# The mixing of a unit stands one step later, next to the scores, in two attention stages

## The chip, the cores and the metric

The kernel runs on one core of one Trainium2 chip. The metric is the device time of one execution in microseconds (us). All tensors are float32; the projections split each operand into a rounded high part and the rest (fp32r) and sum the products.

## The reference

The program is a small vision tower on 64 images of 36 tokens, 192 channels: patch embedding, a causal attention with 12 heads of 64 columns, a block with a norm, an attention with 12 heads of 16 columns and an MLP, a second attention with 12 heads of 16 columns and a distance bias, and a mixture of experts. The change touches the two 16-column attentions only. What one of them computes:

```python
qkv = x @ w_qkv.T + b_qkv                       # x: (64, 36, 192)
q, k, v = qkv.reshape(B, N, 3, 12, 16)...       # 12 heads of 16
scores = einsum('bhnd,bhmd->bhnm', q, k) * 16 ** -0.5 + bias
attn = softmax(scores, axis=-1)
out = einsum('bhnm,bhmd->bhnd', attn, v)        # the mixing
return out.transpose(...).reshape(B, N, 192) @ w_proj.T + b_proj
```

The first of them (named attn2) has no bias in the scores and a layer norm ahead of it; the second (attn3) has the bias.

## The kernel before, in words

Both stages are `narrow_stage` (L563). The 2304 tokens are taken as 32 units of two images (72 tokens), four units to a group, so 8 groups of 288 tokens. Each engine has its program written out by hand, as a loop over 35 steps k; engines meet by semaphores only. Every engine works through its own list in order.

For unit k the work goes through the engines like this:

- TensorE `scores(k)` (L802): 8 matmuls, q against a block-diagonal copy of the keys (tiles keys_a, keys_b; L813). Before the first unit of a group it waits for the 12 transfers that fill these tiles (L806).
- VectorE `take_scores(k)` (L1011): row maximum and, in attn2, the subtraction (L1023, L1025). In attn3 it adds the bias (L1017), takes the maximum (L1021), and GpSimd subtracts (`shift`, L722).
- ScalarE `exponentiate(k)` (L927), VectorE `sum_up(k)` (L1031, L1036), GpSimd `normalise(k)` (L715).
- TensorE `turn(k)` (L817): 4 transposes (L823); ScalarE `copy_turned(k)` (L934) brings them to prob_t.
- TensorE `mix(k)` (L827): 8 matmuls of prob_t with the block-diagonal values (L839, 8 instructions, told as 8 pairs of load and matmul); ScalarE `copy_z(k)` (L944) brings the result to z_t.
- TensorE `project_out(t)` for a token tile t of 128 (L848, L849), VectorE `add_residual(t)` (L1040).

At step k the TensorE issues scores of unit k, the transposes of unit k-2, a share of the next group's input work, the output projection of a finished tile, and last the mixing of unit k-2. The next group's input work is spread over the four steps of a group: transposes of x (L768, L769) at the first, the projections of q and k (L779 to L783, twice) at the second, the third projection and the first values (L795 to L799) at the third, the other values at the fourth.

The key tiles are filled by the SyncE queue (`spread_keys_a`, L646, and `spread_keys_b`, L656). It waits until ScalarE has copied the keys (tile k_a, L911 in attn2 and L913 in attn3, which follows the second of the two projections at a group's second step), issues 8 transfers for keys_a (L653), then 4 for keys_b (L659), then 9 for the values (L673). In attn3 the same queue also loads weights for the last stage (L1800, L1802 each group; ten transfers at L1783 to L1790 once, behind the keys of group 2). Groups are counted from 0 here; "the keys of group 4" are those that unit 16 waits for.

Of the kernel before, what the change touches and what calls it, by code (L numbers as in the profile page):

```python
# [562 lines left out]
def narrow_stage(nc, psum, ident, neg_half, name, h_tok, y_tok, w, out_ws, c2_scale, qk_bias, bias_hk,  # L563
# [4 lines left out]
    groups, units = TOK // WIDE, TOK // UNIT  # L568
# [19 lines left out]
    with Sems(nc, name) as S, ExitStack() as ctx:  # L588
# [29 lines left out]
        def scores_ps(k):  # L618
            return bank(2 + k % 2)[:, 0:HEADS * SEQ].rearrange("p (h n) -> p h n", h=HEADS)
# [139 lines left out]
        def _(pe):  # L759
# [42 lines left out]
            def scores(k):  # L802
                g, u = k // per_group, k % per_group
                if u == 0:
                    pe.wait_ge(S["qk_copied"], 3 * g + 3)
                    pe.wait_ge(S[f"keys_ready{g % 2}"], 16 * 12 * (g // 2 + 1))  # L806
                if k >= 2:
                    pe.wait_ge(S["scores_taken" if bias_hk is not None else "shifted"], k - 1)
                ps = scores_ps(k)
                for q, keys, h0, h1 in ((q_a, keys_a, 0, 8), (qk_b, keys_b, 8, HEADS)):  # L810
                    for a in range(2):
                        at = u * UNIT + a * SEQ
                        last = nc.tensor.matmul(ps[64 * a:64 * a + 64, h0:h1, :], q[g % 2][:, at:at + 64],  # L813
                                                keys[g % 2][:, :, at:at + SEQ], start=True, stop=True)
                last.then_inc(S["scores_done"], 1)

            def turn(k):  # L817
                pe.wait_ge(S["normalised"], k + 1)
                if k >= 2:
                    pe.wait_ge(S["turned_copied"], k - 1)  # L820
                flat = prob[k % 3][:, :, :].rearrange("p h n -> p (h n)")
                for n in range(4):
                    last = nc.tensor.transpose(bank(4 + k % 2)[0:3 * SEQ, n * P:n * P + QP],  # L823
                                               flat[:, n * 3 * SEQ:(n + 1) * 3 * SEQ], ident[0:QP, 0:QP])
                last.then_inc(S["turned"], 1)
# [32 lines left out]
            for k in range(steps):  # L858
                g, j = k // per_group + 1, k % per_group
                if k < units:  # L860
                    scores(k)
                if 2 <= k < units + 2:
                    turn(k - 2)
                if g < groups:
                    if j == 0:
                        transpose_x(g)
                    elif j == 1:
                        project(g, 0)
                        project(g, 1)
                    elif j == 2:  # L870
                        project(g, 2)
                        values(g, 0)
                    else:
                        values(g, 1)
                        values(g, 2)
                for t in ready_tiles(k):
                    project_out(t)
                if 2 <= k < units + 2:
                    mix(k - 2)

        @block.scalar
        def _(act):
            def round_x(g):
                ts = new_tiles(g)
                n, at = len(ts) * P, ring_span(ts)
                act.wait_ge(S["x_transposed"], g + 1)
                if prenorm:
                    ga, gb, ba, bb = norms[g * len(norms) // groups]
                    act.wait_ge(S["x_split"], g)
                    nc.scalar.activation(aff_a[:, 0:n], bank(0)[:, 0:n], ACT.Identity, bias=ba, scale=ga  # L890
                                         ).then_inc(S["x_affine"], 1)
                    nc.scalar.activation(aff_b[:, 0:n], bank(1)[0:DB, 0:n], ACT.Identity, bias=bb, scale=gb
                                         ).then_inc(S["x_affine"], 1)
                    act.wait_ge(S["x_affine"], 2 * g + 2)
                    nc.scalar.activation(a_hi[:, at], aff_a[:, 0:n], ACT.Copy).then_inc(S["x_rounded"], 1)
                    nc.scalar.activation(b_x[0:DB, at], aff_b[:, 0:n], ACT.Copy).then_inc(S["x_rounded"], 1)
                else:
                    nc.scalar.activation(a_hi[:, at], bank(0)[:, 0:n], ACT.Copy).then_inc(S["x_rounded"], 1)
                    nc.scalar.activation(b_x[0:DB, at], bank(1)[0:DB, 0:n], ACT.Copy
                                         ).then_inc(S["x_rounded"], 1)  # L900

            def copy_qk(g, c):
                act.wait_ge(S["qk_done"], 3 * g + c + 1)
                if c == 1 and g >= 1:
                    act.wait_ge(S[f"keys_ready{(g - 1) % 2}"], 16 * 12 * ((g - 1) // 2 + 1))
                if c != 1 and g >= 2:
                    act.wait_ge(S["scores_done"], per_group * (g - 1))
                out = (q_a[g % 2], k_a, qk_b[g % 2])[c][:, 0:WIDE]
                scale = (0.25, 1.0, c2_scale)[c]
                if qk_bias is None:  # L910
                    ins = nc.scalar.activation(out, bank(c % 2)[:, 0:WIDE], ACT.Copy, scale=scale)  # L911
                else:
                    ins = nc.scalar.activation(out, bank(c % 2)[:, 0:WIDE], ACT.Identity,  # L913
                                               bias=qk_bias[:, c:c + 1], scale=scale)
                ins.then_inc(S["qk_copied"], 1)

            def copy_v(g, n):
                act.wait_ge(S["v_done"], 3 * g + n + 1)
                if g >= 1 and n == 0:
                    act.wait_ge(S[f"values_ready{(g - 1) % 2}"], 16 * 9 * ((g - 1) // 2 + 1))  # L920
                m = 3 * SEQ if n < 2 else 2 * SEQ
                nc.scalar.activation(v_tok[0:m, n, :], bank((n + 1) % 2)[0:m, 0:D], ACT.Copy
                                     ).then_inc(S["v_copied"], 1)

            def exponentiate(k):
                act.wait_ge(S["shifted"], k + 1)
                nc.scalar.activation(prob[k % 3][:, :, :], prob[k % 3][:, :, :], ACT.Exp  # L927
                                     ).then_inc(S["exp_done"], 1)

            def copy_turned(k):  # L930
                act.wait_ge(S["turned"], k + 1)
                if k >= 2:
                    act.wait_ge(S["mixed"], k - 1)
                nc.scalar.activation(prob_t[k % 2][:, :, :, :], turned_ps(k)[0:3 * SEQ, :, :, 0:SEQ], ACT.Copy  # L934
                                     ).then_inc(S["turned_copied"], 1)

            def copy_z(k):
                act.wait_ge(S["mixed"], k + 1)
                over = k * UNIT + UNIT - 1 - z_ring
                if over >= 0:  # L940
                    act.wait_ge(S["out_done"], over // P + 1)
                at = (k * UNIT) % z_ring
                n = min(UNIT, z_ring - at)
                ins = nc.scalar.activation(z_t[:, :, at:at + n], z_ps[:, :, 0:n], ACT.Copy)  # L944
                if n < UNIT:
                    ins = nc.scalar.activation(z_t[:, :, 0:UNIT - n], z_ps[:, :, n:UNIT], ACT.Copy)
                ins.then_inc(S["z_copied"], 1)

            round_x(0)
            for c in range(3):  # L950
                copy_qk(0, c)
            for n in range(3):
                copy_v(0, n)
            for k in range(steps):
                g, j = k // per_group + 1, k % per_group
                if 1 <= k <= units:
                    exponentiate(k - 1)
                if 2 <= k < units + 2:
                    copy_turned(k - 2)
                if g < groups:  # L960
                    if j == 0:
                        round_x(g)
                    elif j == 1:
                        copy_qk(g, 0)
                        copy_qk(g, 1)
                    elif j == 2:
                        copy_qk(g, 2)
                        copy_v(g, 0)
                    else:
                        copy_v(g, 1)  # L970
                        copy_v(g, 2)
                if side and j == 1 and g <= groups:
                    side.round_step(act, g - 1)
                if 2 <= k < units + 2:
                    copy_z(k - 2)

        @block.vector
        def _(dve):
# [1109 lines left out]
```

## Time and profile before

| | us |
|---|---|
| Median of 3 runs | 1170.06 |
| Lowest and highest | 1166.44, 1171.95 |
| The profiled execution | 1165.79 |
| Its span in the profile | 1164.0 |
| Mean granted TensorE clock | 0.938 of full speed |
| PE (matmul) busy | 1013.6 (87%) |
| DVE, ACT, POOL busy | 561.9, 395.4, 319.6 |
| attn2: first scores to last projection | about 354 to 496 |
| attn3: the same | about 646 to 803 |

PE is the TensorE with its matmuls, PEld its weight loads (they run beside the matmuls), DVE the VectorE, ACT the ScalarE, POOL the GpSimd, SP the SyncE. A matmul's end is modelled, so successive matmuls overlap in the listing and a busy PE is not a PE at its peak. "Idle before, releaser" is the time in which an engine did nothing ahead of an instruction, and what ended that. The releaser "issue" means that the profile shows nothing that the engine waited for; a wait for a transfer may be put down there.

### The profile page before, as it was taken

How to read it: one execution, taken by the hardware profiler on the slowest of the kernel's cores; microseconds unless marked ns; L12 is line 12 of the kernel's file. 1: busy time of each engine (PE TensorE's matmuls, PEld its weight loads, DVE VectorE, ACT ScalarE, POOL GpSimd, SP SyncE). 2: the span in 40 equal slices, each digit the busy share in tenths (PEclk: the TensorE clock that was granted, in tenths of full speed). 3: DMA queues.
4: the chain of work that ended last, by engine and by line, in shares of the span. 5: the costliest groups of instructions: out<-in, count | busy, mean ns of one | idle time of the engine just before them, and what ended most of it. 6: DMA issues, size and time to landing. Idle time of an engine off the chain costs nothing. (4 is left out here: it accounts for less than half of the span.)

```text
span 1164.0 us, 21593 instructions
## 1 busy us (share of the span) xinstructions
PE 1013.6 (87%) x8306; PEld 925.2 (79%) x8306; DVE 561.9 (48%) x1489; ACT 395.4 (34%) x882; POOL 319.6 (27%) x349
## 2 busy tenths in 40 slices
PE   6879998999847999868998678976999999999997
PEld 6768888888735777758997466865999999999996
DVE  2225454555544666457331355654444454545444
ACT  1245554555413455323442344542212121111110
POOL 4424343443441222224223465663000000000000
PEclk9999999999977899879998898986999999999999
DMA  9711010101001111000000142210000000000000
GB/s 294 219 39 24 24 33 24 33 23 29 29 4 27 26 29 28 16 1 1 1 1 22 48 115 66 65 47 3 1 1 12 1 11 1 11 1 12 1 11 11
DMA packets 40757, 39.08 MB, mean 34 GB/s; under 512 B 21072, under 2 KB 32208, under 8 KB 40656
## 3 DMA queue, kind: packets, MB, share of 16 engines
q1 hardware_dynamic: 38528, 33.38, 10.3%
q10 hardware_dynamic: 2128, 4.34, 1.3%
q8 instruction: 66, 1.08, 0.4%
q14 instruction: 35, 0.29, 0.1%
HBM read 21.76 MB, written 1.77 MB: 20 GB/s over the span
## 5 line engine op out<-in xcount | busy, mean ns | idle before, releaser
L1485 ACT ACTIVATE moe_silu<-psum 128x384 f32<-128x384 f32 x108 | 53.2, 492 | 273.7 <-PE psum L76 266.3
L1389 POOL TENSOR_TENSOR moe_rstd<-moe_var_eps,neg_half 128x3 f32<-128x3 f32 x6 | 5.1, 851 | 349.5 <-DVE moe_var_eps L1584 349.5
L715 POOL TENSOR_TENSOR attn_prob<-attn_prob,attn_recip 100x432 f32<-100x432 f32 x64 | 58.3, 912 | 132.2 <-DVE attn_recip L1036 132.2
L839 PEld LDWEIGHTS psum<-attn_prob_t,attn_values 108*64 108x64 f32 x1024 | 66.6, 214 | 24.5 <-issue 10.5
L839 PE MATMUL psum<-attn_prob_t,attn_values 108*64 108x36 f32 x1024 | 74.1, 293 | 10.5 <-DMA attn_values<-attn_v_tok 6.2
L1555 DVE TENSOR_TENSOR moe_hid_pair<-psum,moe_silu 128x384 f32<-128x384 f32 x72 | 40.1, 557 | 87.3 <-PE psum L76 87.3
L813 PE MATMUL psum<-attn_keys_a,attn_q_a 128*64 128x288 f32 x256 | 51.2, 480 | 35.4 <-issue 23.2
L1571 DVE SCALAR_TENSOR_TENSOR moe_acc<-psum,moe_coef,moe_acc 128x192 f32<-128x192 f32 x144 | 59.7, 418 | 44.9 <-PE psum L1439 44.5
L1439 PE MATMUL psum<-w_dn,moe_hid_pair 128*128 128x192 f32 x288 | 73.4, 337 | 6.3 <-DVE moe_acc L1571 6.3
L72 PE MATMUL psum<-moe_x_a_hi,w_gu_a_hi 128*128 128x384 f32 x216 | 76.2, 353 | 0.0
L235 POOL TENSOR_TENSOR attn_prob_x<-attn_prob,attn_recip 100x864 f32<-100x864 f32 x32 | 52.6, 1643 | 76.4 <-DVE attn_recip L517 76.4
L74 PE MATMUL psum<-moe_x_a_hi,w_gu_a_lo 128*128 128x384 f32 x216 | 72.9, 338 | 0.0
L73 PE MATMUL psum<-moe_x_a_lo,w_gu_a_hi 128*128 128x384 f32 x216 | 72.9, 338 | 0.0
L76 PE MATMUL psum<-moe_x_b,w_gu_b_lo 128*128 128x384 f32 x216 | 72.9, 337 | 0.0
L75 PE MATMUL psum<-moe_x_b,w_gu_b_hi 128*128 128x384 f32 x216 | 72.8, 337 | 0.0
L1031 DVE TENSOR_REDUCE attn_row_sum<-attn_prob 100x12 f32<-100x432 f32 x64 | 38.5, 602 | 63.2 <-ACT attn_prob L927 62.9
L1439 PE MATMUL psum<-w_dn_mid,moe_hid_pair 128*128 128x192 f32 x288 | 69.0, 335 | 0.0
L1236 ACT ACTIVATE mlp_hid<-psum,columns 128x384 f32<-128x384 f32 x72 | 39.9, 581 | 54.2 <-PE psum L76 36.3
L1439 PEld LDWEIGHTS psum<-w_dn,moe_hid_pair 128*128 128x128 f32 x288 | 49.0, 190 | 10.9 <-DVE moe_acc L1571 10.7
L1439 PEld LDWEIGHTS psum<-w_dn_mid,moe_hid_pair 128*128 128x128 f32 x288 | 47.0, 189 | 4.9 <-DVE moe_acc L1571 3.7
L1726 PE MATMUL psum<-embed_w_tok,embed_patches 128*128 128x192 f32 x216 | 39.5, 341 | 10.3 <-DMA embed_w_tok<-in_tok_w 5.8
L1726 PEld LDWEIGHTS psum<-embed_w_tok,embed_patches 128*128 128x128 f32 x216 | 36.4, 197 | 13.1 <-DMA embed_patches<-in_x 7.2
(318 smaller groups left out, 2698.3 us busy)
## 6 DMA issues: line engine op xcount, KB each, us to landing
embed_patches<-in_x SPq DMA_DIRECT2D x18, 384.0 KB, 23.1
attn_v<-attn_v_tok SPq DMA_DIRECT2D x16, 216.0 KB
attn_values<-attn_v_tok SPq DMA_DIRECT2D x96, 27.0 KB
attn_keys_a<-attn_k_a SPq DMA_DIRECT2D x128, 18.0 KB, 1.8
raw_a<-in_w_gu_dram SPq DMA_DIRECT2D x8, 288.0 KB, 3.2
raw_b<-in_w_gu_dram SPq DMA_DIRECT2D x16, 144.0 KB, 3.2
y<-moe_y SPq DMA_DIRECT2D x6, 288.0 KB
attn_keys_b<-attn_qk_b SPq DMA_DIRECT2D x64, 18.0 KB, 1.8
```

What stands on the lines that cost most here:

```text
L72: nc.tensor.matmul(out, w.a_hi[:, cols], x.a_hi[:, toks], start=True, stop=False)
L73: nc.tensor.matmul(out, w.a_hi[:, cols], x.a_lo[:, toks], start=False, stop=False)
L74: nc.tensor.matmul(out, w.a_lo[:, cols], x.a_hi[:, toks], start=False, stop=False)
L75: nc.tensor.matmul(out, w.b_hi[:, cols], x.b[:, toks], start=False, stop=False)
L76: return nc.tensor.matmul(out, w.b_lo[:, cols], x.b[:, toks], start=False, stop=True)
L235: nc.gpsimd.tensor_tensor(prob_x[k % 2][:, :, :, :], prob[k % 3][:, :, :].rearrange("p h (a n) -> p h a n", a=1) .to_broadcast([QP, HEADS, ...
L715: nc.gpsimd.tensor_tensor(pr, pr, recip[k % 2][:, :].rearrange("p (h a) -> p h a", a=1) .to_broadcast([QP, HEADS, SEQ]), ALU.mult).then_in ...
L839: last = nc.tensor.matmul(ps[r:r + 64, n // 2, a * SEQ:(a + 1) * SEQ], v[:, n, :], prob_t[k % 2][:, n, a, :], start=True, stop=True)
L1439: last = nc.tensor.matmul(down_ps(n), hid(gr)[:, c, t * MT:(t + 1) * MT], w, start=(m == 0), stop=(m == len(terms) - 1))
L1485: nc.scalar.activation(silu[c % 2][:, :], bank(2 * (c % 2))[:, 0:MW], ACT.Silu).then_inc(S["silu_done"], 1)
L1571: ins = nc.vector.scalar_tensor_tensor(out=acc[:, t, :], in0=down_ps(n), scalar=scalar, in1=h_tok[:, 3 * i + t, :] if e == 0 else acc[:, t ...
L1726: last = nc.tensor.matmul(out_bank(t), patches[:, t, c, :], w_tok[:, c, :], start=(c == 0), stop=(c == chunks - 1))
```

## The change

In the TensorE's list the mixing moves from the end of step k, where it took unit k-2, to the place right behind the scores of step k, where it takes unit k-3. In the ScalarE's list the copy of its result moves from the end of the step to the place behind the exponential, with the same unit k-3. Nothing else is edited: as many instructions, the same operands, the same semaphores. The lists of DVE, POOL and SP are the same.

```diff
@@ TensorE
                 if k < units:
                     scores(k)
+                if k >= 3:
+                    mix(k - 3)
                 if 2 <= k < units + 2:
                     turn(k - 2)
...
                 for t in ready_tiles(k):
                     project_out(t)
-                if 2 <= k < units + 2:
-                    mix(k - 2)
@@ ScalarE
                 if 1 <= k <= units:
                     exponentiate(k - 1)
+                if k >= 3:
+                    copy_z(k - 3)
                 if 2 <= k < units + 2:
                     copy_turned(k - 2)
...
-                if 2 <= k < units + 2:
-                    copy_z(k - 2)
```

On the TensorE, at the end of a group's last step and the start of the next group in attn2, before and with the change (L799 ends the last values, L813 are scores, L839 is the mixing, L823 the transposes of the probabilities, L768 those of x):

```order
 L799 MATMUL psum<-w_qkv_b_lo,attn_b_x 72x192
-L839 MATMUL psum<-attn_prob_t,attn_values 64x36 x8
-L813 MATMUL psum<-attn_keys_a,attn_q_a 64x288 x2
-L813 MATMUL psum<-attn_keys_b,attn_qk_b 64x144 x2
+L813 MATMUL psum<-attn_keys_a,attn_q_a 64x288 x2
+L813 MATMUL psum<-attn_keys_b,attn_qk_b 64x144 x2
+L839 MATMUL psum<-attn_prob_t,attn_values 64x36 x8
 L823 MATMUL psum<-ident,attn_prob 108x100 x4
 L768 MATMUL psum<-ident,attn_x_hat 128x128
```

The mixing that stood ahead of a group's first scores, and so ahead of their wait for the key tiles, now stands behind them.

On the ScalarE, in the same steps of attn2 (L922 are copies of values, L944 the copy of a mixing, L927 an exponential, L934 the copy of the transposed probabilities, L890 the first work on the next group's x):

```order
-L944 ACTIVATE attn_z_t<-psum 128x2x72
-L927 ACTIVATE attn_prob<-attn_prob 100x432
-L934 ACTIVATE attn_prob_t<-psum 108x288
-L922 ACTIVATE attn_v_tok<-psum 108x192
-L922 ACTIVATE attn_v_tok<-psum 72x192
-L944 ACTIVATE attn_z_t<-psum 128x2x72
-L927 ACTIVATE attn_prob<-attn_prob 100x432
+L927 ACTIVATE attn_prob<-attn_prob 100x432
+L944 ACTIVATE attn_z_t<-psum 128x2x72
+L934 ACTIVATE attn_prob_t<-psum 108x288
+L922 ACTIVATE attn_v_tok<-psum 108x192
+L922 ACTIVATE attn_v_tok<-psum 72x192
```

Each exponential now stands ahead of the copy of a mixing instead of behind it.

## Rows read from the trace of the kernel before

**Rows 1.** Windows, attn2 and attn3 (window, its length, busy us by engine; PEclk).
```profile
354.00:496.00 142.00, 128.00 (x1208) 103.81 (x1208) 83.33 (x205) 65.11 (x170) 33.53 (x38) 0.90 0.10 25
646.00:803.00 157.00, 129.46 (x1208) 104.76 (x1208) 91.64 (x228) 69.78 (x173) 93.40 (x105) 0.87 0.24 63
```
**Rows 2.** Waits in attn2, 354 to 496 (us in total, times, longest).
```profile
PE psum L813 <- issue: 7.8, 7, 1.9
...
PE psum L839 <- ACT attn_prob_t L934: 1.2, 2, 0.7
```
**Rows 3.** Waits in attn3, 646 to 803.
```profile
PE psum L813 <- issue: 15.4, 7, 4.5
...
PE psum L839 <- DMA attn_values<-attn_v_tok: 6.2, 2, 5.6
...
PE psum L839 <- ACT attn_prob_t L934: 2.6, 5, 1.0
...
PE psum L823 <- POOL attn_prob L715: 1.8, 3, 0.7
```
**Rows 4.** Timeline of the SP queue in attn2 (start, us, count of transfers issued).
```profile
414.69 5.01 SPq L653 DMA_DIRECT2D attn_keys_a<-attn_k_a  x8
419.75 2.48 SPq L659 DMA_DIRECT2D attn_keys_b<-attn_qk_b  x4
422.67 8.24 SPq L673 DMA_DIRECT2D attn_values<-attn_v_tok  x9
431.02 5.01 SPq L653 DMA_DIRECT2D attn_keys_a<-attn_k_a  x8
...
446.81 5.00 SPq L653 DMA_DIRECT2D attn_keys_a<-attn_k_a  x8
```
**Rows 5.** Timeline of PE, first scores of groups 2 and 4 in attn2.
```profile
388.58 1.23 PE L813 MATMUL psum<-attn_keys_a,attn_q_a 128*64 128x288 f32 x4 [1.66 <-issue]
...
423.53 0.71 PE L813 MATMUL psum<-attn_keys_a,attn_q_a 128*64 128x288 f32 x4 [0.20 <-issue]
```
**Rows 6.** Timeline of PE, first scores of group 6 in attn3.
```profile
762.08 1.23 PE L813 MATMUL psum<-attn_keys_a,attn_q_a 128*64 128x288 f32 x4 [4.47 <-issue]
```
**Rows 7.** Timeline of ACT, copies of the keys in attn2.
```profile
414.25 0.41 ACT L911 ACTIVATE attn_k_a<-psum 128x288 f32<-128x288 f32 x1 [0.25 <-PE psum L783]
429.79 0.41 ACT L911 ACTIVATE attn_k_a<-psum 128x288 f32<-128x288 f32 x1 [0.26 <-PE psum L783]
446.13 0.41 ACT L911 ACTIVATE attn_k_a<-psum 128x288 f32<-128x288 f32 x1 [0.24 <-PE psum L783]
```
**Rows 8.** Timeline of PE in attn2, a mixing and the scores behind it.
```profile
397.18 1.15 PE L839 MATMUL psum<-attn_prob_t,attn_values 108*64 108x36 f32 x16
...
398.15 0.69 PE L813 MATMUL psum<-attn_keys_a,attn_q_a 128*64 128x288 f32 x4
```
**Rows 9.** Timeline of ACT in attn3, the copy of the keys of group 4.
```profile
714.65 0.50 ACT L913 ACTIVATE attn_k_a<-psum,columns 128x288 f32<-128x288 f32 x1 [0.16 <-PE psum L783]
```
**Rows 10.** Timeline of the SP queue in attn3, the same group.
```profile
716.43 4.99 SPq L653 DMA_DIRECT2D attn_keys_a<-attn_k_a  x8
```
**Rows 11.** Windows from a group's first scores to the end of its second step's projections.
```profile
372.25:378.45 6.20, 6.20 (x60) 5.08 (x60) 3.62 (x8) 3.69 (x9) 1.17 (x2) 1.00 0.15 34
388.58:397.24 8.66, 8.66 (x60) 6.63 (x60) 4.48 (x11) 3.71 (x9) 1.83 (x2) 0.64 0.12 27
423.53:429.75 6.22, 5.86 (x55) 4.66 (x56) 4.29 (x10) 4.19 (x11) 1.58 (x2) 1.00 0.13 29
762.08:770.44 8.36, 8.36 (x60) 6.48 (x60) 4.82 (x12) 2.71 (x7) 2.29 (x3) 0.71 0.21 47
```
**Rows 12.** Timeline of DVE in attn2, scores of unit 28 shifted.
```profile
475.56 0.61 DVE L1025 TENSOR_TENSOR attn_prob<-psum,attn_row_max 100x432 f32<-100x432 f32 x1
```
**Rows 13.** Timeline of ACT in attn2, copy of a mixing, exponential of unit 28.
```profile
477.23 0.20 ACT L946 ACTIVATE attn_z_t<-psum 128x48 f32<-128x48 f32 x1
477.32 0.56 ACT L927 ACTIVATE attn_prob<-attn_prob 100x432 f32<-100x432 f32 x1
```

## The prediction

> **What bounds the kernel now.** I read the windows of the two stages first. In attn2 the PE is busy 128.0 of 142 us, in attn3 129.5 of 157, and no other engine comes near [rows 1]. So the order of work can only matter where the PE stands still, or where its clock is low (0.90 and 0.87 in these windows). The table of waits says where it stands still: at the scores. Seven waits of 7.8 us in attn2 and seven of 15.4 us in attn3 are put down to "issue", the longest 1.9 and 4.5 us [rows 2, 3]. Seven is the number of groups after the first, and the code waits for the key tiles at the first scores of a group.
>
> The timeline of the SP queue says what these waits are for. For group 4 of attn2 the queue issues 8 transfers from 414.69 and 4 more from 419.75 to 422.23 [rows 4]; the scores start at 423.53 after 0.20 us of waiting [rows 5], 1.30 us behind the last issue. I measured that distance for all 14 groups: 1.30 to 1.39 us each time. So the start of a group hangs on the last of 12 issues, whatever the PE does meanwhile. And the first issue hangs on the copy of the keys: this copy ends at 414.25 + 0.41 = 414.66 [rows 7], the queue starts 0.03 us later. The copy itself follows the last projection matmul of the group's second step by 0.25 us of idle ScalarE.
>
> That closes a loop: first scores of a group, PE work up to the second step's projections, copy, 12 issues, landing, first scores of the next group. From the copy's end to the scores it is 423.53 - 414.66 = 8.87 us, in which the PE only fills time.
>
> **The change part by part.** It adds and removes no instruction. What matters is on which side of the projections a mixing stands. Before, between a group's first scores and the second step's projections there is one mixing (end of the first step); with the change there are two (behind the scores of both steps). Behind the projections there were three up to the next group's scores, now two. The total is the same, so the PE reaches the next group's scores no later; but the keys leave one mixing later, and the wait for them grows by that mixing.
>
> *Price of a mixing on that path.* A mixing starts at 397.18, the scores behind it at 398.15 [rows 8]: 0.97 us. Ahead of a mixing or a transpose the weight loads show a gap of about 0.2 us, which the new place may add: upper bound 1.17. I take 1.1.
>
> *Where it counts in attn2.* For group 1 nothing changes: no mixing stands yet ahead of its keys. Groups 2, 3, 4 and 7 have the queue waiting for the copy as group 4 does: 4 x 1.1 = 4.4 us. For group 5 the copy ends at 430.20 [rows 7], but the queue starts at 431.02, since it issues values until 422.67 + 8.24 = 430.91 [rows 4]. 0.8 us of the delay vanish there: 0.3 left. For group 6 the copy ends at 446.54 and the queue starts at 446.81: 0.9 left. Sum 5.6 us.
>
> *Where it counts in attn3.* The queue also carries weights there. For group 4 the copy ends at 715.15 [rows 9] and the queue starts only at 716.43 [rows 10]: 1.28 us of slack swallow the mixing. Groups 3 and 6 have more slack still (this row stands for three). Groups 2, 5 and 7 start within 0.03 us of the copy: 3 x 1.1 = 3.3 us.
>
> Together 8.9 us, with 0.97 or 1.17 for a mixing 7.7 or 9.5.
>
> *The clock.* The windows from a group's first scores to its second step's projections show a second price. The same 60 matmuls take 6.20 us at a granted clock of 1.00 and 8.66 or 8.36 us at 0.64 and 0.71 [rows 11], that is in part at the lower of the levels 1.2 and 2.4 GHz. The two slow ones follow waits of 1.66 and 4.47 us, the one with a wait of 0.20 stays at 1.00 [rows 5, 6, 11]. Of the eight waits over 1.5 us six are followed by such a stretch, of the four below 1.0 us that have such a window none is. With up to 1.1 us more, four groups that ran at full clock and from which the path to the next keys leads (1, 3, 4 and 5 of attn2) have waits of 1.3 to 3.0 us; in attn3 the two at full clock (2 and 5) come ahead of keys with slack. A slow stretch costs about 2 us (8.66 and 8.36 against 6.20). I take two of the four: +4; bounds 0 and +8.
>
> *The exponential ahead of the copy.* At the end of attn2 no keys are left to wait for, and the loop over the units binds. The scores of unit 28 are shifted at 475.56 + 0.61 = 476.17 [rows 12], the exponential starts only at 477.32, behind the copy of a mixing [rows 13]: 1.1 us late. Now it goes first. The last three units gain less each. I take -1.1, bounds 0 and -1.7. In attn3 GpSimd's subtraction comes between: there the last exponentials start right behind it, with the copy long done: 0.
>
> *The mixing's own waits.* 1.2 us in attn2 and 2.6 in attn3 for the copy of the transposed probabilities [rows 2, 3] go away, but most of them lie in the last units, where the next transposes then wait instead, so they bring nothing beyond the term before. The wait for values, 6.2 us in attn3 [rows 3], is one queue that issues ten weight transfers first. The mixing of unit 8 now stands behind the scores of unit 11, but group 3's keys are issued behind these values, so the group starts no sooner: 0.
>
> Sum: 8.9 + 4 - 1.1 = +11.8 us. On the profiled execution (1165.8) this gives 1177.6; that one was 4.3 us under the median. On the median it gives 1181.9, and I say 1182.
>
> The Trainium skill (DMA: Bandwidth & Descriptors, Issuing engines are not separate DMA queues) calls the time a sequencer takes to initiate a DMA usually small relative to the DMA itself. Here it isn't: 12 issues fill 7.5 us of the queue and the landing takes 1.3 [rows 4, 5]. By the page's rule the keys would be there long before the PE asks, and the sum would be the last term alone, -1.1.
>
> **The rivals.**
>
> *The PE is the bound and the total is the same.* For it: 90% busy in attn2 [rows 1], equal instruction lists. Against it: a start fixed at 1.3 us behind an issue in 14 of 14 groups. It would need the projections to keep their time although a mixing is put ahead of them. Then 1170, or 1169 with the last units. The Trainium skill (Perfetto Trace Analysis, Identifying the Most-Contended Engine) points the same way: the engine with the highest occupancy is what to improve, and its work is untouched. Chance 0.14.
>
> *The waits of mixing and turning decide, and the kernel gets faster.* The mechanism is the ScalarE's order: exponentials no longer stand behind a copy that waits for the PE, a mixing no longer waits for a copy just made. If all of 1.2 + 2.6 + 1.8 us [rows 2, 3] and the 6.2 us at the values went, 11.8 us would be gained: 1158. It decides if the keys' issue had slack in most groups; the trace shows slack in five of the twelve that matter. Chance 0.06.
>
> *Longer waits, but no lower clock.* Two waits, 1.9 and 1.7 us, were followed by full clock (the window from 372.25 is one [rows 11]). Then 8.9 - 1.1 = +7.8: 1178. Chance 0.22.
>
> *Lower clock in all four groups.* 8.9 + 8 - 1.1 = +15.8: 1186. Chance 0.16.
>
> **How the numbers follow.** My forecast with part of the clock has 0.42. About 0.5% (5.9 us) is what a measurement of this kernel can tell from no change. Forecast, the no-clock case and the all-clock case are slower by more, except a share of the no-clock case near its lower bound (7.7 - 1.7 = 6.0), which I leave there: slower 0.79, same 0.15, faster 0.06. Within the slower cases the time lies between 1176 and 1188 (upper mixing bound 9.5 with all the clock, and 1.7 us that runs differ by); the range reaches down into the no-change case and a little past the upper end: 1171 to 1191.
>
> **What would show it.** In the changed profile the waits put down to "issue" at the scores grow from 7.8 + 15.4 = 23 us in both stages to about 34 (1.1 more in each of nine groups, 0.3 and 0.9 in two); the first scores of a group still start 1.3 us behind the last key issue; the time from a group's first scores to the copy of the keys grows from 6.3 (423.53 to 429.79) to about 7.4 us at full clock; the SP queue stands idle longer ahead of keys_a; exponentials start right behind the shift; more of the first-step windows have a clock under 1. The step fails if the copy of the keys keeps its distance to the group's first scores, or if the sum of the waits at the scores is what it was.

## The result, and the profile after

| | us |
|---|---|
| Before, median of 20 runs | 1166.97 (1163.07 to 1174.82) |
| After, median of 20 runs | 1174.68 (1169.62 to 1182.62) |
| Ratio after to before | 1.0067, 95% interval 1.0045 to 1.0089 |
| Profiled execution of after | 1181.3, span 1179.5, granted clock 0.918 |

The changed kernel is slower, by 7.7 us (5.2 to 10.4 by the interval). Its profiled execution is one of the slowest of its twenty: the fastest four took 1169.6 to 1171.3 us at a mean granted clock of 0.932 to 0.935, the slowest three 1181.3 to 1182.6 us at 0.918 to 0.923. So the 15.5 us between the two spans (1179.5 and 1164.0) aren't all the change's. In the places where groups start they can be read apart, and there I compare.

First the two stages (the window, its length, busy us of PE, its weight loads, DVE, ACT and POOL, the granted clock, DMA share, GB/s):

```profile
358.00:508.00 150.00, 129.64 (x1208) 109.52 (x1208) 82.44 (x204) 65.81 (x170) 33.59 (x38) 0.84 0.10 23
662.00:819.00 157.00, 129.23 (x1208) 108.40 (x1208) 92.61 (x228) 70.09 (x173) 93.50 (x105) 0.83 0.23 63
```

The same 1208 matmuls as in [rows 1]; the clock is 0.84 and 0.83 where it was 0.90 and 0.87. Next what the PE waits for (us in total, times, longest), in attn2 from 340 to 508:

```profile
PE psum L813 <- issue: 16.1, 7, 3.7
...
PE psum L839 <- ACT attn_prob_t L934: 0.5, 1, 0.5
```

and in attn3 from 640 to 820:

```profile
PE psum L813 <- issue: 20.9, 7, 5.0
```

Against [rows 2, 3] the wait at a group's first scores grew from 7.8 to 16.1 and from 15.4 to 20.9 us, 23.2 to 37.0 together; the mixing's wait for the copy of the probabilities shrank.

The SP queue in attn2 still does what [rows 4] show: 8 issues, 4 issues, 9 issues of values (start, length, line, transfer, count).

```profile
431.77 8.01 SPq L673 DMA_DIRECT2D attn_values<-attn_v_tok  x9
440.20 5.01 SPq L653 DMA_DIRECT2D attn_keys_a<-attn_k_a  x8
445.25 2.48 SPq L659 DMA_DIRECT2D attn_keys_b<-attn_qk_b  x4
447.99 7.91 SPq L673 DMA_DIRECT2D attn_values<-attn_v_tok  x9
```

The copy of the keys that releases it, on ACT:

```profile
439.76 0.41 ACT L911 ACTIVATE attn_k_a<-psum 128x288 f32<-128x288 f32 x1 [0.26 <-PE psum L783]
```

The copy ends at 440.17, the queue starts at 440.20, the last issue ends at 447.73, and the next group's scores start at 449.05: 1.32 us behind, as before. The loop of the prediction is unchanged; it has become longer. Where, the PE's timeline shows (start, length, instruction, idle time before and what ended it), here for the group that starts at 432.63:

```profile
432.63 0.71 PE L813 MATMUL psum<-attn_keys_a,attn_q_a 128*64 128x288 f32 x4 [1.14 <-issue]
...
433.39 1.06 PE L839 MATMUL psum<-attn_prob_t,attn_values 108*64 108x36 f32 x16
...
435.10 0.27 PE L769 MATMUL psum<-ident,attn_x_hat 128*64 128x128 f32 x1
...
436.08 1.03 PE L839 MATMUL psum<-attn_prob_t,attn_values 108*64 108x36 f32 x16
...
438.12 0.40 PE L779 MATMUL psum<-attn_a_hi,w_qkv_a_hi 128*128 128x288 f32 x1 [0.52 <-DVE attn_b_x L1008]
```

In the kernel before, the same stretch of the group that starts at 423.53 [rows 5]:

```profile
425.14 0.27 PE L769 MATMUL psum<-ident,attn_x_hat 128*64 128x128 f32 x1
425.47 1.15 PE L839 MATMUL psum<-attn_prob_t,attn_values 108*64 108x36 f32 x16
...
428.16 0.40 PE L779 MATMUL psum<-attn_a_hi,w_qkv_a_hi 128*128 128x288 f32 x1 [0.30 <-DVE attn_b_x L1008]
```

From a group's first scores to the copy of its successor's keys it was 6.26 us (423.53 to 429.79) and is 7.13 (432.63 to 439.76). In three pieces: first scores to the last transpose of x, 1.61 before, 2.47 after; last transpose of x to the first projection, 3.02 before, 3.02 after; projection to copy, 1.63 and 1.64. But for 0.01 all of the 0.87 us lies in the first piece. The middle piece holds one mixing in either kernel (the first step's before, the second step's after) and takes the same time, but in neither is it the PE's work that fills it: the PE waits at its end for the VectorE, 0.30 us before and 0.52 after. The first of these waits was in the trace of before, and I had not read it.

What fills the middle piece in attn2 is one chain over two engines. ACT, then DVE, of after:

```profile
435.41 0.57 ACT L890 ACTIVATE attn_aff_a<-psum,columns 128x256 f32<-128x256 f32 x1
435.88 0.55 ACT L892 ACTIVATE attn_aff_b<-psum,columns 64x256 f32<-64x256 f32 x1
436.46 0.42 ACT L895 ACTIVATE attn_a_hi<-attn_aff_a 128x256 fp32r<-128x256 f32 x1
436.78 0.40 ACT L896 ACTIVATE attn_b_x<-attn_aff_b 64x256 fp32r<-64x256 f32 x1
```

```profile
437.21 0.43 DVE L1007 TENSOR_TENSOR attn_a_lo<-attn_aff_a,attn_a_hi 128x256 fp32r<-128x256 f32 x1 [2.34 <-ACT attn_b_x L896]
437.65 0.42 DVE L1008 TENSOR_TENSOR attn_b_x<-attn_aff_b,attn_b_x 64x256 fp32r<-64x256 f32 x1
```

In attn3 it is otherwise. No norm is applied there, so two of the ScalarE's four operations on x are missing. In the kernel before, in a group at full clock that starts at 682.23, the VectorE is done with x at 685.68 and the PE gets to the projection only at 686.86, without a wait for it:

```profile
685.26 0.42 DVE L1008 TENSOR_TENSOR attn_b_x<-psum,attn_b_x 64x256 fp32r<-64x256 f32 x1
```

```profile
683.83 0.27 PE L769 MATMUL psum<-ident,h_tok 128*64 128x128 f32 x1
...
686.86 0.38 PE L779 MATMUL psum<-attn_a_hi,w_qkv_a_hi 128*128 128x288 f32 x1
```

So the middle piece, 3.03 us here too, is filled by the PE's own list in attn3.

### The profile page after: what moved, and what is told of

It is laid out like the page before. It is cut to its first block and busy times, and to the rows that moved or that the text cites. A ratio compares the mean times of both kernels' runs of the same rounds, so it can differ in the third digit from the quotient of the medians.

```text
span 1179.5 us, 21593 instructions
## 1 busy us (share of the span) xinstructions
PE 1021.7 (87%) x8306; PEld 941.3 (80%) x8306; DVE 561.6 (48%) x1489; ACT 396.8 (34%) x882; POOL 320.0 (27%) x349
## 5 line engine op out<-in xcount | busy, mean ns | idle before, releaser
L813 PE MATMUL psum<-attn_keys_a,attn_q_a 128*64 128x288 f32 x256 | 54.5, 509 | 48.6 <-issue 37.0
L839 PEld LDWEIGHTS psum<-attn_prob_t,attn_values 108*64 108x64 f32 x1024 | 68.9, 213 | 6.1 <-DMA attn_values<-attn_v_tok 2.7
L839 PE MATMUL psum<-attn_prob_t,attn_values 108*64 108x36 f32 x1024 | 68.4, 284 | 4.0 <-DMA attn_values<-attn_v_tok 2.4
L813 PEld LDWEIGHTS psum<-attn_keys_a,attn_q_a 128*64 128x64 f32 x256 | 14.9, 155 | 63.0 <-issue 61.5
L1439 PEld LDWEIGHTS psum<-w_dn,moe_hid_pair 128*128 128x128 f32 x288 | 49.0, 190 | 10.9 <-DVE moe_acc L1571 10.7
```

Of the source, the lines that this page charges most:

```text
L839: last = nc.tensor.matmul(ps[r:r + 64, n // 2, a * SEQ:(a + 1) * SEQ], v[:, n, :], prob_t[k % 2][:, n, a, :], start=True, stop=True)
L1439: last = nc.tensor.matmul(down_ps(n), hid(gr)[:, c, t * MT:(t + 1) * MT], w, start=(m == 0), stop=(m == len(terms) - 1))
```

## The experiments

Ten kernels were run, one of them twice, in batches that shared runs of the kernel before. Ratios are to before, with 95% intervals. "Scores to keys" is the time from a group's first scores to the copy of the next group's keys, at full clock unless said.

**The ScalarE's half alone.** Mixing stays where it was; its copy comes one step later, behind the exponential.

```diff
                 if 1 <= k <= units:
                     exponentiate(k - 1)
+                if k >= 3:
+                    copy_z(k - 3)
...
-                if 2 <= k < units + 2:
-                    copy_z(k - 2)
```

> ScalarE's half of the change alone: the copy of a mixing stands behind the exponential, one step later, and the mixing itself stays at the end of the step on the TensorE. Theory (the mixing that moved onto the path between a group's first scores and the copy of its keys costs the time): no mixing is on that path more than before, so 0 to -2 us, and the waits put down to issue at the scores (L813) stay at 23 us in both stages. Rival A (the ScalarE's new order costs the time): +6 to +9 us. Rival B (a mixing costs more wherever it stands next to scores, about 0.12 us in each of 64 places): 0.

Measured: 1167.09 against 1168.96 us, 0.9983 (0.9953 to 1.0012); waits at the scores 8.5 + 14.5 = 23.0 us, as before. The order on the ScalarE neither makes the loss nor, to within 0.5%, gives anything.

**The mixing behind the scores only in a group's first step.** ScalarE as in the change.

```diff
+                if k >= 3 and k % per_group != 0:
+                    mix(k - 3)
                 if k < units:
                     scores(k)
+                if k >= 3 and not (k % per_group != 0):
+                    mix(k - 3)
```

> The change, but on the TensorE only the mixing of a group's first step stands behind the scores; in the other three steps it stands ahead of them, where it ran before. That puts two mixings between a group's first scores and the copy of the next keys, as the whole change does. Theory: the whole loss, +6 to +9 us against before, waits at the scores about 37 us as in the changed kernel. Rival A: also +6 to +9. Rival B: a quarter of the places, so about +2 us and waits near 23 us.

Measured: 1176.56 against 1168.96 us, 1.0072 (1.0044 to 1.0100); waits 15.2 + 21.8 = 37.0 us. Scores to keys is 7.12 us (429.39 to 436.51):

```profile
429.39 0.71 PE L813 MATMUL psum<-attn_keys_a,attn_q_a 128*64 128x288 f32 x4 [1.28 <-issue]
430.14 1.07 PE L839 MATMUL psum<-attn_prob_t,attn_values 108*64 108x36 f32 x16
...
431.86 0.27 PE L769 MATMUL psum<-ident,attn_x_hat 128*64 128x128 f32 x1
...
434.88 0.40 PE L779 MATMUL psum<-attn_a_hi,w_qkv_a_hi 128*128 128x288 f32 x1 [0.30 <-DVE attn_b_x L1010]
```

The whole loss comes from one of four places, and again 3.02 us pass between the last transpose of x and the projection.

**The complement: behind the scores everywhere but in a group's first step.**

```diff
+                if k >= 3 and k % per_group == 0:
+                    mix(k - 3)
                 if k < units:
                     scores(k)
+                if k >= 3 and not (k % per_group == 0):
+                    mix(k - 3)
```

> The other three quarters of the change: only the mixing of a group's first step stays ahead of the scores (and so ahead of the wait for the keys), the others stand behind the scores. One mixing between first scores and the copy of the keys, as before. Theory: none of the loss, 0 to -2 us, waits at the scores 22 to 24 us. Rival A: +6 to +9. Rival B: three quarters of it, +6 us.

Measured: 1169.87 against 1168.96 us, 0.9995 (0.9969 to 1.0022); scores to keys 6.27 us (428.24 to 434.51); waits 11.1 + 16.7 = 27.8 us, more than the 22 to 24 expected. The distance came out as expected. The time, 0.9 us above before where 0 to 2 us below was expected, can't be told from either; the sum of waits did not come out; where its 4 us come from I have not followed up.

**The second step's mixing behind the projections too.** If each mixing ahead of the keys counts, one fewer should gain.

```diff
                     elif j == 1:
                         project(g, 0)
                         project(g, 1)
+                        if k >= 3:
+                            mix(k - 3)
```

> As mix_cover, but the mixing of a group's second step stands behind the two projections (and its copy behind the copies of q and the keys), so that no mixing stands between a group's first scores and the copy of the next keys. Theory: the keys leave 1.1 us earlier than before where their queue has no slack; the waits at the scores fall from 23 to about 17 us and the time by 3 to 6 us against before. Rival A: +6 to +9. Rival B: about +3 us.

Measured: 1168.97 against 1168.96 us, 1.0000 (0.9973 to 1.0026). A miss. The waits in attn2, 340 to 512, of this kernel:

```profile
PE psum L779 <- DVE attn_b_x L1014: 11.0, 8, 3.4
...
PE psum L813 <- issue: 4.4, 4, 1.9
```

and of before:

```profile
PE psum L813 <- issue: 7.8, 7, 1.9
...
PE psum L779 <- DVE attn_b_x L1008: 6.0, 4, 3.4
```

The scores wait 3.4 us less and the projections 5.0 us more. Scores to keys is 6.25 us (376.96 to 383.21), as with the mixing inside; the last transpose of x starts at 378.56 and the projection at 381.58, once more 3.02. The mixing behind the transposes of x had cost nothing in attn2, since it lay beside the chain through x, and taking it away left the PE idle there. In attn3 taking it away did bring the keys forward: in its group 4, at full clock, scores to keys is 5.13 us (730.60 to 735.73) where it is 5.73 with the mixing inside (728.69 to 734.42 in the kernel with the ScalarE's half alone). The middle piece shrank from 2.51 to 1.90 us, and only then did the PE wait for x there:

```profile
732.20 0.27 PE L769 MATMUL psum<-ident,h_tok 128*64 128x128 f32 x1
...
734.10 0.40 PE L779 MATMUL psum<-attn_a_hi,w_qkv_a_hi 128*128 128x288 f32 x1 [0.26 <-DVE attn_b_x L1014]
```

The SP queue did not use it: it reached these keys 3.6 us behind their copy. This run made me give up the step "a mixing more ahead of the keys is a mixing later" in that general form, and the next two test what takes its place.

**The first step's mixing behind the transposes of x.** The change, with both mixings under the chain through x.

```diff
                     if j == 0:
                         transpose_x(g)
+                        if k >= 3:
+                            mix(k - 3)
...
                     if j == 0:
                         round_x(g)
+                        if k >= 3:
+                            copy_z(k - 3)
```

> The change, with the mixing of a group's first step put behind the transposes of the next group's x instead of ahead of them (its copy behind the rounding of x). Two mixings still stand between a group's first scores and the copy of the keys. Theory of the chain through x: from the last transpose of x to the first projection it takes 3.02 us in the kernel before and in the changed one, filled by the ScalarE's four and the VectorE's two operations on x; only what stands ahead of the transposes of x moves the keys, and in the changed kernel the PE still waits 0.52 us at the projections. With both mixings behind x the PE has 0.97 us more to do under a cover of 0.52: first scores to copy of the keys 6.25 + 0.45 = 6.70 us at full clock, no wait for the split of x there, ratio to before 1.002 to 1.005. Theory of the prediction (each mixing between the first scores and the keys counts in full, wherever it stands): 7.1 us, ratio 1.007. Theory that only the mixing ahead of the transposes of x counts: 6.25 us, ratio 1.000.

Measured: 1188.91 against 1167.84 us, 1.0173 (1.0138 to 1.0208), far above what any of the three theories gave. Two groups of attn2 on the PE:

```profile
395.87 0.71 PE L813 MATMUL psum<-attn_keys_a,attn_q_a 128*64 128x288 f32 x4 [3.00 <-issue]
...
400.60 1.01 PE L848 MATMUL psum<-w_o,attn_z_t 128*128 128x192 f32 x2 [0.97 <-ACT attn_z_t L948]
...
434.62 0.71 PE L813 MATMUL psum<-attn_keys_a,attn_q_a 128*64 128x288 f32 x4 [1.50 <-issue]
...
438.62 1.15 PE L839 MATMUL psum<-attn_prob_t,attn_values 108*64 108x36 f32 x16 [0.28 <-ACT attn_z_t L946]
...
440.04 0.38 PE L779 MATMUL psum<-attn_a_hi,w_qkv_a_hi 128*128 128x288 f32 x1
```

In the second of these, at full clock, the keys are copied at 441.66: 7.04 us behind the scores. The projections no longer wait for x, but the second mixing waits 0.28 us for the copy of the first one, which I had put behind the rounding of x on the ScalarE. Without that wait it would be 6.76, near the 6.70 of the chain. In the first group an output projection ahead of the second scores waits 0.97 us for the same copy. So the edit brought a wait of its own. The traces say where most of the 21 us lie. From the first scores of the first group to those of the last, attn2 took 134.3 us (119.3 before) and attn3 139.1 (133.6 before). In attn2 nearly all of it is scores to keys of groups 1, 2, 5 and 6, the four in whose first step an output projection stands behind the mixing and waits 0.92 to 0.97 us for its copy: they took 11.4, 11.8, 8.4 and 11.5 us in place of 6.2, 8.7, 6.2 and 7.9; groups 3 and 4 took 0.5 and 0.8 more. Group 5 ran at full clock in both kernels, and there the edit cost 2.2 us; the other three ran at a granted clock of 0.58 to 0.62. No run parts the wait from the clock, so how much each costs stays open. What the run shows is that a copy behind the rounding of x is dear, and that the PE's wait for x is gone.

**The transposes of x sooner.** The kernel with the second mixing behind the projections, and the transposes of x ahead of the turning of the probabilities.

```diff
+                if g < groups and j == 0:
+                    transpose_x(g)
                 if 2 <= k < units + 2:
                     turn(k - 2)
...
+                if g < groups and j == 0:
+                    round_x(g)
                 if 2 <= k < units + 2:
                     copy_turned(k - 2)
```

> The kernel whose second-step mixing stands behind the projections (it gained nothing), with the transposes of x in a group's first step ahead of the turning of the probabilities, and the rounding of x ahead of its copy. Theory of the chain through x: the transposes of x come 0.4 to 0.5 us sooner behind the first scores, 3.02 us later the projections start: first scores to copy of the keys 6.25 - 0.45 = 5.8 us at full clock; the waits for the split of x shrink, those put down to issue at the scores shrink or stay. The SP queue issues 15.7 us of transfers in each group of 16.4 us, so little of it can be used: ratio to before 0.995 to 1.000. Theory that the PE's own work sets the time from first scores to keys: the total is the same, 6.25 us stays, ratio 1.000.

Measured: 1166.53 against 1167.84 us, 0.9977 (0.9957 to 0.9998). On the PE:

```profile
426.93 0.69 PE L813 MATMUL psum<-attn_keys_a,attn_q_a 128*64 128x288 f32 x4
...
428.18 0.27 PE L769 MATMUL psum<-ident,attn_x_hat 128*64 128x128 f32 x1
...
431.20 0.40 PE L779 MATMUL psum<-attn_a_hi,w_qkv_a_hi 128*128 128x288 f32 x1 [1.04 <-DVE attn_b_x L1014]
```

3.02 us again, and scores to keys is 5.91 us (426.93 to 432.84) where 5.8 was expected and 6.25 would have stayed under the rival. Of the seven groups behind the first, four in attn2 now start without a wait put down to issue. In attn2 the chain through x is what the distance hangs on; the gain in time is small, as expected.

**Four of the twelve key issues from the ScalarE's queue.** If the loop through the SP queue is what makes the place of a mixing matter, a shorter loop should take that away. On the kernel before, on the changed one, and on the complement above:

```diff
                     if j == 1:
                         spread_keys_a(g)
-                    if j == 2:
-                        spread_keys_b(g)
...
                         copy_qk(g, 2)
+                        spread_keys_b(g)
                         copy_v(g, 0)
```

> The kernel before, with the 4 keys_b transfers of each group issued by the ScalarE's queue right behind its copy of qk_b, instead of by the SP queue behind the 8 of keys_a. Theory (12 issues in a row on one queue set the start of a group): copy of the keys to the next first scores falls from 8.9 to the PE's own work of about 8 us, the waits at the scores of both stages from 23 us to under 6, the time by 12 to 22 us, since the SP queue of attn3 is relieved too and fewer stretches have a low clock. Rival (the wait is for the landing of the transfers, not for their issue): the waits stay, time within 3 us of before. Second rival (the ScalarE's own work is delayed by 2.5 us of issues per group): +3 to +8 us.

> The changed kernel with the same edit. Theory: with the wait for the keys gone, the place of the mixing costs nothing; the difference to kb_before is 0 to -3 us (what the exponential's earlier place brings), where it was +7.8 us with the keys on one queue. Rival (a mixing behind the scores costs time of itself): +6 to +9 us against kb_before. So theory: 12 to 24 us under before.

> mix_cover with the same edit: the mixing of a group's first step ahead of the scores, the others behind. Theory: as kb_before and kb_after within 3 us, since no placement matters once nobody waits for the keys.

Measured, against 1168.45 us: before with the edit 1143.42 us, 0.9774 (0.9745 to 0.9804); the changed kernel with it 1141.12 us, 0.9765 (0.9736 to 0.9793); the complement with it 1138.24 us, 0.9753 (0.9718 to 0.9789). Two expectations were missed on the good side: 25.0 and 27.3 us were gained where 12 to 22 and 12 to 24 were forecast. The changed order is now 2.3 us below the old one, where it was 7.7 above: the loss is gone. The complement is 5.2 us below the old order, outside the 3 expected, but with six runs a side (means 3.5 apart, 2.0 their standard error) this is not told from nothing. Most of the gain is in attn3, where the SP queue loads weights as well: from the first scores of the first group to those of the last, before with the edit takes 117.6 us there in place of 133.6, and 114.6 in attn2 in place of 119.3. From the copy of the keys to the next first scores attn2 takes 7.8 to 9.4 us where about 8 was forecast, but none of these scores waits any more: the PE's own work sets the distance. The waits at the scores of the changed kernel with the edit, in attn2 (345 to 500) and then in attn3 (630 to 800), L803 being the scores there:

```profile
PE psum L803 <- issue: 1.5, 5, 0.5
```

```profile
PE psum L803 <- issue: 9.2, 6, 3.9
```

37.0 us have become 10.7. The price is on the ScalarE, whose own queue now issues ahead of the copies of the values:

```profile
412.11 2.52 ACTq L912 DMA_DIRECT2D attn_keys_b<-attn_qk_b  x4
```

**The same four issues one copy later, and the complement again.**

```diff
                         copy_qk(g, 2)
-                        spread_keys_b(g)
                         copy_v(g, 0)
+                        spread_keys_b(g)
```

> kb_cover, with the ScalarE's 4 keys_b issues behind its copy of the first values instead of ahead of it. In the two profiles with the earlier place the TensorE waits 5 to 10 us in all for the copy of values, held up by 2.5 us of issues per group. Theory: these waits shrink, the keys still land before the TensorE asks: 0 to 4 us under kb_cover, 29 to 34 under before. Rival (the keys now land too late): waits at the scores come back, +2 to +6 us against kb_cover.

> kb_cover again beside it on the same chip, for the comparison: 26 to 32 us under before.

Measured, against 1166.91 us: 1137.20 us, 0.9738 (0.9700 to 0.9776), and 1139.23 us, 0.9753 (0.9718 to 0.9788). The PE's waits for the copy of the values (L785) are 2.2 us in attn2 and 1.6 in attn3, once each, against 3.2 in four waits and 5.2 in five in the complement with the earlier place; the two times aren't told apart. Either is about 2.5% faster than the kernel before and beats the changed one by about 3%.

## Why the prediction came out as it did

*Slower: right, by the mechanism named.* 7.7 us measured against 11.8 forecast. The start of a group still hangs on the last of twelve issues (1.32 us behind it), and the first issue on the copy of the keys (0.03 us). Taking four of the twelve off that queue removed most of the waits and with them the loss: that the loop is the cause is shown.

*The step that was mis-sized: the price of a mixing, 1.1 us.* It measured 0.87 and 0.88 in the two groups of attn2 that ran at full clock in both profiles, and 0.77 in the one of attn3 (6.23 to 7.00 us). The bounds 0.97 and 1.17 both missed. The working counted mixings between the first scores and the copy of the keys, and supposed the PE to be what fills that distance. In attn2 it isn't all of it. Behind the last transpose of x, 3.02 us go through the ScalarE and the VectorE, in before, in after and in five experiments (3.02 or 3.03 each time). There the PE's work counts only ahead of that transpose, where the change puts one mixing, 0.99 us (433.39 to the turning at 434.38), and saves a gap: turning started 0.89 us behind the scores in before (423.53 to 424.42), the mixing starts 0.76 us behind them now. 0.99 - 0.13 = 0.86. The mixing in the second step, which the prediction counted as the one already there, is free in attn2. So in attn2 the count of one came out right for another reason than given, by luck. In attn3, whose chain through x is shorter, the PE's list does fill the distance, and the reason given holds.

*Where it counts.* With 0.88 the slack that the prediction read stays: attn2 4 x 0.88 for groups 2, 3, 4 and 7, 0.88 - 0.79 = 0.09 for group 5, 0.88 - 0.24 = 0.64 for group 6, together 4.25; attn3 3 x 0.88 = 2.64, if the price of attn2 is taken for it. Sum 6.9 us in place of 8.9. In the changed profile the SP queue starts within 0.03 us of the copy for all seven groups of attn2, and has slack of 6.91 and 1.29 us for groups 3 and 6 of attn3. Group 4's slack there, 1.28 us, which was to swallow the mixing, has gone to 0.03: it was swallowed, and more.

From the first scores of the first group to those of the last, attn2 took 119.3 us in the profiled execution of before (354.63 to 473.93) and 127.3 in that of after (358.39 to 485.66): 8.0 more, of which 4.25 are these. Attn3 took 133.6 (646.99 to 780.57) and 134.2 (662.26 to 796.45): 0.6 more, not 2.64. The three groups that count there, 1, 4 and 6, took 7.85, 8.25 and 8.39 us from first scores to the copy of the keys in before and 8.32, 8.66 and 8.74 in after. That is 1.2 us more and not 2.64; all three ran partly at the lower clock in both profiles (0.59 to 0.78), so a mixing's price can't be read there. Against it stand the twelve issues behind the copy in group 1, which took 8.3 us in before and 7.5 in after, and the other groups, whose stretches changed by up to 1 us either way. These are two executions, and no run isolates any of it.

The mixing's wait for the values fell in attn3, from 6.2 us [rows 3], nearly all of it in one place of before, to 2.4, in the same place of after:

```profile
698.17 1.18 PE L839 MATMUL psum<-attn_prob_t,attn_values 108*64 108x36 f32 x16 [5.59 <-DMA attn_values<-attn_v_tok]
```

```profile
PE psum L839 <- DMA attn_values<-attn_v_tok: 2.4, 1, 2.4
```

The prediction had taken 0 for this wait, and for the reason it gave that was right: between the first scores of groups 2 and 3 the SP queue issues without a pause (680.96 to 706.38 before, 696.03 to 721.89 after), and this stretch took 25.5 us before and 25.9 after.

*The clock.* Forecast: two of four groups of attn2 (1, 3, 4 and 5) lose it, 2 us each. The windows from first scores on, after:

```profile
374.85:383.62 8.77, 8.77 (x76) 7.58 (x78) 3.75 (x9) 4.01 (x10) 0.55 (x1) 0.73 0.12 27
393.52:403.14 9.62, 9.62 (x76) 7.93 (x78) 4.60 (x11) 4.07 (x11) 0.92 (x1) 0.66 0.10 24
412.98:420.60 7.62, 6.40 (x63) 5.30 (x63) 2.41 (x5) 3.84 (x10) 0.20 (x1) 0.77 0.13 29
432.63:439.73 7.10, 6.57 (x72) 5.76 (x73) 3.66 (x9) 3.78 (x10) 1.60 (x2) 1.00 0.14 32
449.05:456.14 7.09, 7.09 (x76) 6.21 (x78) 3.85 (x10) 4.01 (x10) 1.32 (x2) 1.00 0.14 31
```

Groups 1 and 3 (374.85 and 412.98, behind waits of 3.65 and 1.96 us) fell below 1.00, groups 4 and 5 (waits of 1.14 and 1.45) stayed there. Group 1's window was 6.20 us at full clock [rows 11] and is 8.77; less 0.87 for the mixing, 1.7 us are the clock's. The whole of attn2 leaves 8.0 - 4.25 = 3.75 us for the term that was put at 4. That is one execution, and a slow one. Of the median's 7.7 us the mixings take 4.25 + 2.64 = 6.9 or, with attn3 as measured, 4.9; so between 0.8 and 2.8 us are left for the clock less the last units, forecast at +2.9. No edit isolates the clock, so this term is not settled closer than that. The rest of the 15.5 us between the two spans lies elsewhere, 3.8 us ahead of attn2 and 2.4 in the MLP between the stages, where the instructions are the same.

*The last units.* Forecast -1.1 (0 to -1.7). The half alone gave 0.9983, with an interval that holds 1. In the changed profile unit 28's exponential starts at 489.43, still 0.8 us behind the shift (1.1 before), now behind the copy of turned probabilities. From the last group's first scores to the last projection attn2 took 21.6 us before and 22.7 after, now with one mixing more in the stretch and at a clock of 0.65 in place of 0.80. So the profile shows no gain there, and neither it nor the half run bears out the 1.1 us.

*The rivals.* "The total is the same" fell by the distance itself and by 1.0067. Its one argument, that the projections keep their time although a mixing is put ahead, is what happened to the second mixing in attn2, and not to the first. "ScalarE order decides" fell with its half run alone. By the time alone, +7.7, the case without lower clock (+7.8) would have won; but it reached that with a mixing too dear and no clock, where the trace shows two groups that lost theirs.

*What would show it.* Waits at the scores were to grow from 23 to about 34 us: 37.0. Scores to keys from 6.3 to 7.4: 7.13. Exponentials were to start right behind the shift: not in the last units. The time said, 1182, is 7 us over the median, 4 of which are the sum's excess (11.8 for 7.7) and 3 the starting point, whose median over 20 runs was 1166.97 where three runs had given 1170.06.

The Trainium skill (DMA: Bandwidth & Descriptors, Issuing engines are not separate DMA queues) calls the time that a sequencer takes to initiate a DMA usually small relative to the DMA itself. Here it isn't. Measured, four issues moved from a queue that had 21 a group (24 in attn3, with the weights) gave 2.3% of the kernel. With each at about 0.62 us (7.49 us for 12, [rows 4]) initiation was the longest single piece of the loop, against 1.3 us from the last issue to the scores.

## What to carry to other kernels

When work is moved on an engine, don't count what stands between two events; find the chain that joins them, across engines, and ask on which side of its first link the moved work lands. An idle time of 0.30 us ahead of an instruction, put down to another engine, is the sign that work ahead of it is free up to that much, and that the engine's own sum is not the distance. Look for it in every stage: the same code had the chain on the path in attn2 and off it in attn3. And where the order of work matters only because a queue of issues ends last, shortening the queue is worth more (2.3 to 2.6% here) than any order (0.7%).

## What the runs showed of the hardware

An issue of one such transfer costs its engine's sequencer about 0.62 us on either engine: 2.48 us for four on the SP queue, 2.52 us for the same four on the ScalarE's, where they hold up its copies.

Twenty executions of one program spread from 1169.6 to 1182.6 us, and roughly in the order of their mean granted clock, from 0.935 down to 0.918. With twenty runs a side a difference of 7.7 us is known to some 2.5 us.

Behind a group's first scores the next operation on the PE starts 0.75 to 0.76 us later if it is a mixing and 0.88 to 0.89 us later if it is a turning, in the seven groups at full clock that I compared.
